# Cross attention on one core: the products with the values done for two key tiles at every second step

## The reference

```python
q = x @ Wq + bq
kv = y @ Wkv + bkv                     # y: 1601 x 96 per batch
k, v = jnp.split(kv, 2, axis=-1)       # 16 heads of 8 columns each
attn = jnp.einsum('bhqd,bhkd->bhqk', q, k) * scale
attn = jax.nn.softmax(attn, axis=-1)
out = jnp.einsum('bhqk,bhkd->bhqd', attn, v)
return out @ Wo + bo
```

## Time and profile before

| | |
|---|---|
| time, median of 3 runs | 1873.82 us (1869.31 to 1875.78) |
| profiled execution: span from its first to its last instruction | 1871.2 us |
| cross attention in it, first to last exponential | 363.6 to 1153.7 us |
| TensorE busy over the span | 1655.1 us (88%) |
| VectorE, ScalarE, GpSimd busy | 1179.3, 859.6, 415.5 us |

### The profile page before, as it was taken

The page is one execution under the profiler, slowest core; times in us unless marked ns, Lnnn a source line. Parts: engine busy times, 40 slices in busy tenths (PEclk is TensorE's granted clock), DMA queues, the critical chain, the costliest instruction groups (busy, mean ns, idle before and its releaser), DMA issues. The chain is left out here.

```text
span 1871.2 us, 34901 instructions
## 1 busy us (share of the span) xinstructions
PE 1655.1 (88%) x11429; PEld 962.9 (51%) x11429; DVE 1179.3 (63%) x2634; ACT 859.6 (46%) x1294; POOL 415.5 (22%) x499
## 2 busy tenths in 40 slices
PE   2677776799998999999999997999999999499998
PEld 1343443244444444444444443788888888344443
DVE  4655532668676776768687783677667765355554
ACT  1333323166666656566666665333334333133443
POOL 4000002030201102030303001443343332033331
PEclk9878886699999999999999998999999999699999
DMA  4212112513132323232232210000000000000001
GB/s 112 64 38 65 37 35 78 96 69 54 35 76 46 93 46 93 46 93 46 71 55 74 50 16 8 2 1 0 0 0 0 0 0 1 6 16 21 21 21 34
DMA packets 87510, 75.69 MB, mean 40 GB/s; under 512 B 23700, under 2 KB 77364, under 8 KB 86452
## 3 DMA queue, kind: packets, MB, share of 16 engines
q1 hardware_dynamic: 87380, 73.96, 17.7%
HBM read 43.25 MB, written 30.42 MB: 39 GB/s over the span
## 5 line engine op out<-in xcount | busy, mean ns | idle before, releaser
L1152 DVE TENSOR_REDUCE b_chunk_max<-psum 128x1 f32<-128x400 f32 (+1 forms) x1024 | 545.3, 570 | 215.1 <-PE psum L1367 207.1
L1290 ACT ACTIVATE b_prob<-psum 128x1024 f32<-128x1024 f32 (+1 forms) x416 | 425.9, 1024 | 255.4 <-PE psum L1404 247.9
L1367 PE MATMUL psum<-k_stack,q_stack 128*128 128x400 bf16 (+1 forms) x1024 | 320.6, 347 | 30.0 <-DMA k_stack<-b_k_scratch 10.7
L1376 PE MATMUL psum<-b_prob,b_v_aug 128*32 128x256 f32 (+1 forms) x3328 | 267.9, 394 | 2.6 <-PE psum L1319 1.7
L1404 PE MATMUL psum<-q_stack,k_stack 128*128 128x256 bf16 (+1 forms) x1664 | 255.0, 276 | 16.2 <-issue 16.0
L1404 PEld LDWEIGHTS psum<-q_stack,k_stack 128*128 128x128 bf16 (+1 forms) x1664 | 146.5, 100 | 136.9 <-issue 71.6
L1367 PEld LDWEIGHTS psum<-k_stack,q_stack 128*128 128x128 bf16 x1024 | 100.0, 98 | 200.3 <-DVE b_chunk_max L1152 171.2
L2064 DVE TENSOR_TENSOR e_hg<-e_gl,e_gate 128x512 f32<-128x512 f32 x128 | 128.2, 1020 | 108.7 <-ACT e_gl L2045 74.6
L1695 ACT ACTIVATE c_prob<-psum,c_mneg 128x128 f32<-128x128 f32 x128 | 47.0, 368 | 229.6 <-DVE c_mneg L1636 229.6
L2045 ACT ACTIVATE e_gl<-psum,b1T 128x512 f32<-128x512 f32 x128 | 87.8, 687 | 139.8 <-PE psum L2092 114.3
L2079 PE MATMUL psum<-e_hg,e_w 128*128 128x512 f32 x256 | 131.9, 598 | 8.9 <-DVE e_hg L2064 8.9
(11 more groups left out here) (221 smaller groups left out, 2154.7 us busy)
## 6 DMA issues: line engine op xcount, KB each, us to landing
k_stack<-b_k_scratch SPq DMA_DIRECT2D x32, 600.4 KB, 10.3
b_k_scratch<-b_kparts SPq DMA_DIRECT2D x7, 1200.8 KB, 4.4
b_k_scratch<-b_kparts SPq DMA_DIRECT2D x7, 800.5 KB, 6.1
b_ctx<-in_ctx SPq DMA_DIRECT2D x8, 576.0 KB
e_w<-in_L_ffn_re_w SPq DMA_DIRECT2D x62, 64.0 KB, 1.8
a_scratch<-a_parts SPq DMA_DIRECT2D x16, 192.0 KB, 2.1
k_stack<-a_scratch SPq DMA_DIRECT2D x16, 192.0 KB, 4.7
q_stack<-b_q_scratch SPq DMA_DIRECT2D x32, 96.0 KB, 2.3
```

The source lines that it names most:

```text
L1152: nc.vector.tensor_reduce(out=chunk_max[:, half, q, column4(hh), c:c + 1], in_=psum[:, 2 + u % 2, 0:w], axis=AX.X, op=ALU.max).then_inc(ma ...
L1290: nc.scalar.activation(prob[0:k, buf, :].rearrange("p (a c) -> p a c", a=2), psum[0:k, 4 + 2 * buf:6 + 2 * buf, :], ACT.Exp, scale=HD ** - ...
L1367: nc.tensor.matmul(psum[:, 2 + u % 2, 0:hi - lo], queries_of(qst, h, slice(q * P, q * P + P)), keys_of(kst, h, slice(lo, hi)), start=True, ...
L1376: last = nc.tensor.matmul(pv[32 * hh:32 * hh + 32, :], v_aug[0:k, kt, g * GH + hh, :], prob[0:k, buf, c:c + T], start=(kt == 0), stop=(kt ...
```

## The change

The values of two tiles are multiplied together. In steps 2, 4, ..., 12 TensorE does the values of the two tiles before (0 and 1 in step 2, and so on), in the odd steps none, and in step 0 the last tile (12) of the group before, as it was. `b_prob` has four buffers in place of two, and ScalarE's wait for `pv_done` is for four steps back. The waits before the first product of a group move from step 1 to step 2 with it.

```diff
+PBUFS = 4
+
+def values_of_step(n):
+    if n == 0:
+        return [KT - 1]
+    return [n - 2, n - 1] if n % 2 == 0 else []
...
-        prob = sb("b_prob", [P, 2, GH * T])
+        prob = sb("b_prob", [P, PBUFS, GH * T])
...
-                    wait(act, pv_done, T_.now("step", 2))
-                    k, buf = tile_rows(n), (T_.n["step"] - 1) % 2
-                    nc.scalar.activation(prob[0:k, buf, :].rearrange("p (a c) -> p a c", a=2),
+                    wait(act, pv_done, T_.now("step", PBUFS))
+                    k, buf, pbuf = tile_rows(n), (T_.n["step"] - 1) % 2, (T_.n["step"] - 1) % PBUFS
+                    nc.scalar.activation(prob[0:k, pbuf, :].rearrange("p (a c) -> p a c", a=2),
...
-            def values():
-                g, kt, buf, back = pending.pop()
+            def values(back):
+                g, kt, buf = pending.pop(0)
                 pe.wait_ge(exp_done, T_.now("step", back))
...
-                    if n == 1 and not first:
+                    if n == 2 and not first:
                         pe.wait_ge(pv_copied, T_.now("group", -1))
-                    if n == 1 and r == 3:
+                    if n == 2 and r == 3:
                         pe.wait_ge(v_placed, T_.up("placed", 2 if first else 1))
-                    if n == 1 and r == 1:
+                    if n == 2 and r == 1:
                         pe.wait_ge(v_placed, T_.now("placed"))
...
-                    if pending:
-                        values()
-                    pending.append((g, n, buf, 1))
+                    for kt in values_of_step(n):
+                        if pending:
+                            values(1 if n == 0 else n - kt)
+                    pending.append((g, n, (T_.n["step"] - 1) % PBUFS))
...
-            pending[0] = pending[0][:3] + (0,)
-            values()
+            values(0)
```

## The result

The changed kernel takes 1903.3 us (median; before 1874.2 us), 1.55% more: the ratio is 1.0155, 95% interval 1.0133 to 1.0176. The profiled execution has a span of 1904.1 us, 32.9 more than the one before; it was the slowest of the four runs (1905.9 us).

A forecast was written before the change was run, and what follows sets the result against it. TensorE was taken to lead the cross attention, partly waiting for VectorE's reductions. 37 us saved against about 80 us of new waits gave +42.4; 1871.2 + 42.4 + 2.6 = 1916 us, range 1896 to 1932.

The forecast's parts named there:

- the worked pair of steps 5 and 6: Hand-made order of three and two units in a plain group: units wait for reductions, the pair gets 0.49 us longer.
- the rival of the bursts: Rival in the experiments: paired bursts themselves cost; with short reductions, 20 to 30 us slower than before; no chance given.
- PEld <- b_chunk_max: Sign in the trace: wait of the units' weight loads for VectorE's reductions, to rise by about 70 us.
- the price of the first tile in a paired burst: TensorE's time for the first of two tiles' values, taken as 0.48 us, so a paired burst is 1.05.
- the bound: Lower limit for the first tile of a paired burst: 0.43 us, streaming alone; the sum is then +33 us.
- the last, without units: The very last group, where nothing is coupled to VectorE: 0.5 us shorter.
- An odd step can't be shorter than 1.03: Claim on ScalarE: exponentials last 1.02 us each, and two scores issued early only queue them.
- PEld <- issue: Sign in the trace: entries of this wait ahead of the values' matmuls, to be about halved.
- The four buffers at nothing: Four buffers for exponentials, with ScalarE's wait for four steps back, were costed at nothing.
- The drains decide: Rival: VectorE keeps pace, only TensorE's 37 us saved remain, 1837 us; decides below 0.19 of new waits per pair; chance 0.07.
- A balance: Rival: new waits of a pair near 0.19 if reductions queue better than at 0.51, no change, 1874 us; chance 0.05.
- No gain inside the pair: Rival: first tile of a pair costs 0.57, sum +58, 1932 us; with a new entry +78, 1952, chance 0.03.

The follow-up runs named there:

- e1: The kernel before with four buffers for exponentials and the wait for four steps back, product order unchanged: 1876.5 us, ratio to before 1.0009.
- e3: The changed kernel with each unit's VectorE reduction over 64 of its 400 columns: 1810.1 us, ratio to before 0.9665.
- e5: The changed kernel with the same 32 units of a group spread differently over the 13 steps: 1872.8 us, ratio to before 0.9986.
- e2: The kernel before with each unit's VectorE reduction over 64 of its 400 columns: 1824.3 us, ratio to before 0.9726.
- e4: The changed kernel with unit 0 ahead of the scores in odd steps: 1889.2 us, ratio to before 1.0077.
- e6: The kernel before with its units spread differently over the steps: 1877.2 us, ratio to before 1.0015.
- e8: The kernel before with units, scores and items placed anew inside the steps and the units spread differently: 1876.0 us, ratio to before 1.0010.
- e10: The kernel of e6 with the norm's scaling on VectorE moved from step 2 to step 1: 1866.9 us, ratio to before 0.9965.
- e12: The kernel of e8 with the norm's scaling moved to step 1: 1865.8 us, ratio to before 0.9953.

## Why the prediction was right, and by how much not

**The mechanism and the sign** hold. Nearest to the trace: the worked pair of steps 5 and 6 has unit 2 wait for the reduction of unit 0 and unit 1 for that of unit 2, at 1.44 and 2.46 behind the scores; these are the two waits at 771.50 and 772.50, 1.45 and 2.45 behind the scores at 770.05. No unit of the trace starts less than 1.00 behind the one two before, which was to be the sign of an error. The short reductions turned the sign, as the theory needs and the rival of the bursts does not.

One of the signs was too large: "PEld <- b_chunk_max" was to rise by about 70 us and rose by 50 (145.7 to 195.5). The sum behind it fares better. Two single bursts and one entry took 2 x 0.57 + 0.10 = 1.24, a paired burst takes 1.00, so 192 x 0.24 = 46 us were saved, and the stage still got 30.3 longer. That makes some 76 us of new waits, an estimate from these rows; the prediction has about 80.

**The size** was 42.4 us, measured 29 (32.9 in the profiled execution). That lies inside the range, but well below the forecast. The step that was off is the price of the first tile in a paired burst. I took 0.48, twice the spacing of passes in a single burst, and kept 0.43, streaming alone, as the bound. In the trace the pair starts at 772.78 and the next weight load is at 773.78: 1.00 and not 1.05, as in each of the 186 bursts that the trace holds with all their sixteen matmuls. So the first tile costs 1.00 - 0.57 = 0.43. The sixteen matmuls take 1.07 in all and the last of them 0.38, so it starts at 0.69 and its pass at 0.67, not at 0.72: if the first pass behind the entry takes 0.24 as in a single burst, the next two follow at (0.67 - 0.24) / 2 = 0.215. With the bound the same sum gives +33. (At the other end, 192 x 0.09 more than +42.4 is +60, where the prediction has +58.) That the profiled span is +32.9 is in part luck: between the first and the last exponential the difference is 30.3, another 1.0 lies ahead of them and 1.6 behind the stage, where nothing was changed. Of the 2.8 us that the corrected sum has too much in the stage, 1.7 are in the groups r = 1; why is open.

By group, each measured from its first exponential to the next one's:

| group | forecast | forecast with 0.43 | measured |
|---|---|---|---|
| r = 0, keys' preparation | +0.67 | +0.37 | +0.1 to +1.0, mostly +0.3 |
| r = 1 | +1.10 | +0.80 | +0.2 to +0.7, mostly +0.6 |
| r = 2, plain | +1.84 | +1.54 | +1.46 |
| r = 3, output | +1.86 | +1.56 | +1.2 to +2.1 |
| the last, without units | -0.5 | -0.5 | -0.62 |

The pairs of a plain group measured +0.31, +0.31, +0.43, +0.31, -0.08 and +0.19, the one without a loss being steps 9 and 10, as forecast. Such a group takes 23.28 us in all (forecast 23.5); its exponentials start 0.9 to 1.6 and 2.1 to 2.7 us apart in turn, where 1.0 and 2.4 were forecast. The spread in r = 3 lies at the loop's end between two batches, from the last exponential of one to the first of the next: 5.2 to 5.7 us before, 5.4 to 6.2 after. Why it varies was not tried.

**Smaller steps.** "An odd step can't be shorter than 1.03" was wrong: two exponentials that are queued start 0.92 apart (x2 in 1.94, each 1.02), since the second begins before the first has ended. What that changes in the sum was not worked out. The entries ("PEld <- issue" for the values) were to halve: 85.2 to 33.9, more than half. VectorE's waits for units rose from 180.1 to 210.2. The four buffers at nothing: right, by e1.

**The rivals.** "The drains decide" has its sign when VectorE is fast (e3), with 14 us in place of 37; its point of decision, waits of a pair under 0.19, was not tried. A balance came only with another spread of the units (e5), and not for the rival's reason: five reductions in a row still take 2.68. "No gain inside the pair" is refuted by the 1.00 us.

**What the prediction's model did not have.** For the changed kernel the forecast was 13 us too high (1916, measured 1903.3), and for e2, e3, e4 the model was good to 3. For the kernel before it promised 11 and 27 us (e6, e8) that did not come. It held only TensorE, VectorE and ScalarE, and two things outside it were found: VectorE beside GpSimd, worth the 10 us of e10 and e12, and the keys' load, a wait of 10 us in e8. Before, the two instructions were just clear of GpSimd's, and the load cost one wait of 1.0 us: both were close by without counting. They don't make up all of the 27 us, as the plain groups of e8 show.

## What to carry to other kernels

A long piece of work on the leading engine can be the pause in which the engine that feeds on it catches up. Merging two of them saves their entries, but the buffers between the engines must carry the other one over the doubled pause; here two psum buffers (0.51 + 0.57 = 1.08 us of reductions) stood against 1.10 us of burst and entry plus scores. A third buffer was not tried; what was tried is less work for VectorE (e3) and other places for the units (e4, e5). Before merging, write the order out with start-to-start distances and look which unit waits for which buffer. And moving work between steps is a change to every engine's queue: look at what each moved instruction will then run beside, and which load it will then be ahead of.

## What the runs showed of the hardware

- Behind a change from 128-column to 32-column weights, the first pass of four column strips (256 columns, float32, one of two instructions per matmul) took 0.24 us and the following ones 0.215; two tiles in one burst took 1.00 us in all 186 bursts that the trace has whole. Entry cost 0.10 us and exit 0.33 us from the last pass to the next weight load.
- A VectorE `tensor_scalar` of 128 x 128 float32 took 0.34 us alone and 0.93 to 1.19 us beside GpSimd's `tensor_tensor` of 128 x 400; reductions from psum beside it kept their 0.57.
- Queued exponentials of 128 x 1024 start 0.92 us apart though each lasts 1.02.
